# Attention plus mixture-of-experts layer on one core: the store of x2's rows moved behind the loads in the sync queue's step, and one Silu chunk of the shared layer moved ahead of the last tile's columns on ScalarE

## The reference

```
x = x + gamma * attention(layernorm(x), ctx, ctx)      # 8 heads, 4 batches of 512 rows x 512 columns
xn = layernorm(x)
shared = (silu(xn @ sw_gate) * (xn @ sw_up)) @ sw_down  # inner width 1408
routed = sum over the 2 best of 8 experts of their gated layer, weighted
x = x + routed + sigmoid(xn @ shared_gate_w) * shared
```

## Time and profile before

| what | value |
|---|---|
| median of 3 runs | 927.85 us (922.9 to 928.9) |
| the profiled execution | 931.65 us |
| its span, first to last instruction | 929.9 us |
| TensorE busy | 863.5 us, 93% of the span |
| VectorE, ScalarE, GpSimd busy | 570.5, 505.5, 442.8 us |
| attention stage | to about 289 us |
| shared layer | to about 650 us, routed experts to the end |

### The profile page before, as it was taken

The page is one execution under the profiler, slowest core; times in us unless marked ns, Lnnn a source line. Parts: engine busy times, 40 slices in busy tenths (PEclk is TensorE's granted clock), DMA queues, the critical chain, the costliest instruction groups (busy, mean ns, idle before and its releaser), DMA issues.

```text
span 929.9 us, 13754 instructions
## 1 busy us (share of the span) xinstructions
PE 863.5 (93%) x4624; PEld 715.8 (77%) x4624; DVE 570.5 (61%) x819; ACT 505.5 (54%) x862; POOL 442.8 (48%) x422
## 2 busy tenths in 40 slices
PE   4988898988986999999999999999999999999993
PEld 3666666666665888888888888888889999999992
DVE  4987888888762553442121212113989999999991
ACT  3886788778754332112111111112778888888881
POOL 5464666677450000004333000000589999999983
PEclk9998999999997999999999999999999999999996
DMA  9112223133234331400032002553945343434442
GB/s 104 47 35 86 85 80 135 57 113 113 80 125 136 103 102 46 136 1 1 2 136 25 1 0 91 187 187 105 336 103 91 69 89 69 83 75 83 76 68 35
DMA packets 63236, 81.24 MB, mean 87 GB/s; under 512 B 15369, under 2 KB 34825, under 8 KB 63186
## 3 DMA queue, kind: packets, MB, share of 16 engines
q1 hardware_dynamic: 53426, 60.14, 21.2%
q0 software_dynamic: 9760, 20.49, 12.3%
HBM read 53.01 MB, written 27.60 MB: 87 GB/s over the span
## 4 chain that ended last, share of the span: by engine, by line
PE 74%; POOL 11%; issue 7%; DVE 3%; ACT 2%; DMA 2%; POOLq 0%; SPq 0%; DVEq 0%; ACTq 0%
PE scores L1359 9%; PE scores L1360 9%; PE scores L1361 9%; PE bank L1373 4%; PE bank L1374 4%; PE bank L1375 4%; PE scores L1224 3%; PE bank L1459 3%; PE bank L1460 3%; PE bank L1461 3%; PE scores L1435 3%; PE scores L1437 3%; PE scores L1436 3%; PE bank L1435 3%; PE bank L1437 2%
## 5 line engine op out<-in xcount | busy, mean ns | idle before, releaser
L1016 DVE TENSOR_TENSOR sg<-scores,sg 128x512 f32<-128x512 f32 x44 | 30.4, 692 | 218.4 <-PE scores L1361 202.6
L1359 PE MATMUL scores<-x_hl,wsp 128*128 128x512 f32 x352 | 138.1, 392 | 0.0
L1360 PE MATMUL scores<-x_hl,wsp 128*128 128x512 f32 x352 | 137.8, 391 | 0.0
L1361 PE MATMUL scores<-x_hl,wsp 128*128 128x512 f32 x352 | 137.5, 391 | 0.0
L615 POOL DMA_INDIRECT slot_rows<-msrc,posi x32 | 36.1, 1129 | 184.6 <-PE scores L1361 178.2
L630 POOL DMA_INDIRECT xg<-x_normed_rows,meta x39 | 39.3, 1007 | 160.0 <-PE scores L1383 141.7
L789 ACT ACTIVATE sg<-scores 128x512 f32<-128x512 f32 x44 | 26.3, 598 | 160.2 <-PE scores L1361 160.2
L936 DVE TENSOR_TENSOR ptl<-bank,pth 128x512 fp32r<-128x512 f32 x128 | 87.7, 686 | 27.2 <-ACT pth L690 26.7
L690 ACT ACTIVATE pth<-bank 128x512 fp32r<-128x512 f32 x128 | 76.7, 599 | 43.2 <-PE bank L1233 42.5
L684 ACT ACTIVATE pb<-scores,negmax 128x512 f32<-128x512 f32 x128 | 88.1, 694 | 13.0 <-DVE negmax L926 13.0
L796 ACT ACTIVATE hh<-sg 128x512 fp32r<-128x512 f32 x44 | 27.8, 632 | 115.9 <-DVE sg L1016 100.9
(11 more groups left out here) (175 smaller groups left out, 2235.4 us busy)
## 6 DMA issues: line engine op xcount, KB each, us to landing
wex<-in_L_ffn_w_gate SPq DMA_DIRECT2D x8, 704.0 KB, 4.3
wex<-in_L_ffn_w_up SPq DMA_DIRECT2D x8, 704.0 KB, 6.1
xb<-in_x SPq DMA_DIRECT2D x16, 256.0 KB, 3.5
cn<-in_ctx SPq DMA_DIRECT2D x16, 256.0 KB, 3.0
x_rows<-xb SPq DMA_DIRECT2D x16, 256.0 KB, 2.0
x_normed_rows<-x2n SPq DMA_DIRECT2D x16, 256.0 KB, 2.3
x_normed_transposed<-x2T SPq DMA_DIRECT2D x16, 256.0 KB, 3.2
x_hl<-x_normed_transposed SPq DMA_DIRECT2D x4, 1024.0 KB, 5.2
```

The lines of the kernel that those rows point to most:

```text
L1359: te.matmul(bk[:, :], hi, xhi, start=(h == 0), stop=False)
L1360: te.matmul(bk[:, :], hi, xlo, start=False, stop=False)
L1361: ins = te.matmul(bk[:, :], lo, xhi, start=False, stop=(h == HC - 1))
```

## The change

In SyncE's step, `store_rows(i - 1)` moves from the first place to behind `load_x(i + 4)`. On ScalarE, `silu_hi(0, 0)` and `hidden_hi(0, 0)` move to between step 17 and step 18, ahead of the waits for the stores; the loop over the chunks leaves them out. Nothing is added or removed otherwise; the two helper functions are only defined earlier.

```
             def step(i):
-                if there(i - 1):
-                    store_rows(i - 1)
                 if there(i - 3):
                     store_normed(i - 3)
                 if there(i + 2):
                     paced(i - 1, 8)
                     load_values(i + 2)
                 if there(i - 3):
                     store_columns(i - 3)
                 if there(i + 4):
                     paced(i, 3)
                     load_x(i + 4)
+                if there(i - 1):
+                    store_rows(i - 1)
...
-            over_tiles(step)
+            for i in range(-4, NT + 2):
+                step(i)
+            silu_hi(0, 0)
+            hidden_hi(0, 0)
+            for i in range(NT + 2, NT + 3):
+                step(i)
...
             for c in range(SC):
-                silu_hi(0, c)
+                if c > 0:
+                    silu_hi(0, c)
                 if c + 2 < SC:
                     weights_hi(c + 2)
                 if c == 5:
                     tokens_hi(1, 1)
-                hidden_hi(0, c)
+                if c > 0:
+                    hidden_hi(0, c)
```

More of the change, by code:

```diff
@@ L769, in step @@
                     values_hi(i + 1)
[L770 to L780, removed]
             def silu_hi(b, c):
@@ L796, in hidden_hi @@
                 sc.activation(hh[p][:, :], sg[p][:, :], ACT.Copy).then_inc(a_hh, 1)
+            for i in range(-4, NT + 2):
+                step(i)
+            silu_hi(0, 0)
+            hidden_hi(0, 0)
+            for i in range(NT + 2, NT + 3):
+                step(i)
+            act.wait_ge(e_lg, NT)
+            act.wait_ge(g_x2n, NT)
+            act.wait_ge(a_lg, NT)
+            for q in range(2):
+                act.wait_ge(st_x2[q], 16 * NI)
+                act.wait_ge(st_x2n[q], 16 * NI)
+                act.wait_ge(st_x2T[q], 16 * NI)
+            act.wait_ge(st_pad, 32)
             for c in range(SC):
-                silu_hi(0, c)
+                if c > 0:
+                    silu_hi(0, c)
                 if c + 2 < SC:
```

## The result

| what | before | after |
|---|---|---|
| median | 925.38 us (920.69 to 928.9, 4 runs) | 897.67 us (896.54 to 899.42, 4 runs) |
| the profiled execution | 931.65 us | 899.42 us |
| its span | 929.9 us | 897.7 us |

The ratio is 0.9705, 95% interval 0.9652 to 0.9758: the changed kernel is 3% faster.

A forecast was written before the change was run, and what follows sets the result against it. Bound: an attention-stage loop through GpSimd, whose key cast waits 3.1 us for a late context load. Gains 27.2 + 2.4 = 29.6 us take the span from 929.9 to 900.3, 902.1 with surroundings; forecast 901 us, range 893 to 915.

The forecast's parts named there:

- The circle: Attention step's dependency loop through GpSimd, TensorE, ScalarE, VectorE: loses the 3.1 us context-load wait, 15.6 becomes 12.5 us.
- What is late next: a step of 13.95 us, TensorE bound: Attention stage: with GpSimd's load wait gone, TensorE's own work sets a step of about 13.95 us.
- The steps behind `first_tokens`: Four attention steps with more GpSimd work: low keys about 0.35 us late each, 1.4 us in all.
- The sum for the attention stage: 23.5 us of TensorE waits plus 5.1 for three slow-clock steps, minus 1.4: 27.2 us gained.
- The clock part: Attention stage: excess of three slow-clock steps, 5.1 us regained; bounds 0 to 5.1.
- The border: Between attention and experts: earlier Silu cuts TensorE's idle time from 7.19 to 4.8 us, 2.4 gained; range 0.7 to 5.4.
- I take zero: Behind the pause after the last logits: no change counted for half-speed products, where 3 us might return or 1.7 go.
- The low end of 893: Bottom of the forecast range: takes in the median's whole 3.8 us and a 5.4 us gain between attention and experts.
- The rival "VectorE becomes the bound": Attention stage: VectorE, busy 13.29 us a step, sets steps of 14.7 to 15 us; 915 or so; chance 0.15.
- The hidden load: Attention stage: GpSimd's next wait absorbs the gain or something equally long replaces it; 925 to 928 us; chance 0.08.
- GpSimd's collisions: Attention stage: moved GpSimd instructions each held 1.5 us by VectorE, making the kernel slower, about 945 us; chance 0.04.
- The rule on the shared ports: VectorE instructions with two SBUF inputs lock out GpSimd; large steady-step operations have at most one, so 13.95 us steps stay.

The follow-up runs named there:

- experiment 3: Kernel before with only the context tile's load moved ahead of the row store: 898.77 us, ratio 0.9728.
- experiment 4: Kernel before with the normed store, column store and load of x moved ahead of the row store, the context load left behind it: 913.1 us, ratio 0.9882.
- experiment 5: Kernel before with each tile's eight router-logit products issued twice: 925.95 us, ratio 1.0023.
- experiment 6: Changed kernel with each tile's eight router-logit products issued twice: 905.72 us, ratio 0.9803 against the kernel before.
- experiment 10: Changed kernel with VectorE's row statistics of x2 issued twice a step, the first into a spare tile: 897.95 us, ratio 0.9720 against the kernel before.
- experiment 7: Changed kernel with the two `first_tokens` instructions moved to where GpSimd waits for VectorE's variance: 894.43 us, ratio 0.9663 against the kernel before.
- experiment 2: Changed kernel with the row store back in its old place, so only the Silu's move against the kernel before: 921.7 us, ratio 0.9987.
- experiment 1: Kernel before with only the row store's move in SyncE's step, Silu in its old place: 899.02 us, ratio 0.9729.
- experiment 8: Changed kernel with the loads of weight chunks 2 and 3 issued before SyncE's step 18: 891.63 us, ratio 0.9635 against the kernel before.
- experiment 11: Kernel before with the row store's move and chunks 2 and 3 loaded before step 18, Silu in its old place: 894.27 us, ratio 0.9670.
- experiment 9: Changed kernel with `first_tokens` in GpSimd's gap, chunks 2 and 3 loaded and chunk 2 cast ahead of step 18: 888.43 us, ratio 0.9613 against before.

## Why the prediction was right

901 us was forecast with a range of 893 to 915; 897.67 was measured.

*The circle.* Right. The key cast's wait went to nothing, the waits for x2n vanished, and no slow-clock step is left between 66 and 232 us. Experiments 3 and 4 show that it is the context load and nothing else that SyncE's reordering moved; experiment 5 shows that TensorE had room before. The load went out 6.2 us into the step, where some 7 were forecast.

*What is late next: a step of 13.95 us, TensorE bound.* The mechanism was right (experiments 6 and 10), the size a little off: 13.61. I had taken TensorE's busy time from steps with waits, 13.91. In a step without waits it is 13.6; each of the two waits had added some 0.15 us to the busy time. The eight ordinary steps of before are 15.66 us in the mean, so each lost 2.05 us through its waits, of which the sum had counted only the time that TensorE stood idle, 1.77 in the mean. That is some 0.28 us too little in each of twelve steps, 3.4 us.

*The steps behind `first_tokens`.* The term was 1.4 us, at 0.35 each. They took 14.28 instead of 13.61, 2.7 us in all, so 1.3 us was missing here. The cause named was right, as experiment 7 shows. That 13.95 + 0.35 = 14.30 comes so near to 14.28 is luck: the two misses cancel.

*The sum for the attention stage* was 27.2; the two profiled executions differ by 29.65 between the row stores. With the two misses above it would have been 27.2 + 3.4 - 1.3 = 29.3. The clock part of 5.1 us is one of that execution: in experiment 2, with the old order, three steps took 16.1, 16.4 and 17.6 us instead of 19.6, 17.2 and 17.4, only the last of them with a clock below 1.00, and the stage 229.69 instead of 234.18. That is how the median moved by 27.7 us and the spans by 32.2, and probably in part why the runs of before scatter over 8 us and those of after over 3. By the medians the store's move brings 25.1 us (experiment 1) and not 27.2. So the closeness of 901 to 897.67 is partly luck: the waits were counted too low, the clock part is more than a usual execution loses, and the two err in opposite directions.

*The border.* 2.4 us were forecast, 2.2 us is the difference of the means over ten traces, and the two profiled executions differ by 1.72. TensorE idles 0.27 + 5.29 = 5.56 us there instead of the 4.8 forecast; chunk 2 landed 6.0 us after its first issue instead of 5.1, and between 5.1 and 5.8 in experiments 2, 6, 7 and 10; the trace doesn't say why. A stretch at the lower clock just ahead of the border is in both and cancels: from the last row store to the last column store 12.69 us after and 12.65 before, against 11.05 to 11.08 in experiments 1 to 4. "I take zero" for the clock behind the pause was right here, the products from 266.42 on ran at half speed too (0.63 us each), for 4.9 us where it had been 6.1. What the forecast did not have is that in experiments 2, 6, 7 and 10 the clock was down for the first down products already, as in experiment 2 above.

*The range.* The low end of 893 is 902.1 - 3.8 - 5.4, but 2.4 of the 5.4 are in the 902.1 already; its terms give 895.3. The measured median lies above either.

*The rival "VectorE becomes the bound"* fell with experiment 10. It had been argued from busy 13.29 of 15.70; with 13.5 of 13.6 the engine still held nobody up in these steps. *The hidden load* fell with experiments 1 and 3. *GpSimd's collisions:* the key cast takes 0.61 us after as before, x2n 0.76, so the moved instructions are not held. The rule on the shared ports was not put to a test of its own: VectorE's maximum at 157.88, which the prediction gave as agreeing, reads its input from PSUM, and none of VectorE's large operations beside the moved ones has two SBUF inputs.

## What to carry to other kernels

In a queue of transfers with waits of their own, a load that somebody needs early must not stand behind a store that waits for the end of the round. Look for an engine that is half idle and yet in the chain, and follow the chain once round. When a wait goes, take what is left from a step that has no waits: busy time beside a wait is too long. And where two waits end close together, taking one away may show little until the other goes as well; the traces of experiments 8 and 11 show this, the run times leave it open.

## What the runs showed of the hardware that was not expected

TensorE's busy time by the profile includes some 0.15 us per wait that isn't work: the same products take 13.9 us with two waits in the step, 13.7 with one (behind `first_tokens`) and 13.6 without. The rows of single products agree with it. Behind 302.6 in the kernel before a product's row is 0.39 us long while the next one starts after 0.23 us (302.66, 302.89); in front of a wait nothing covers the last 0.16 us of a row. These ends are modelled by the profiler, so this says how to read a profile and not how long the products really ran.

Two `BATCH_NORM_STATS2` in a row overlap a little by their rows: in experiment 10 the second started 0.61 us behind the first (95.35 and 95.96), though each row is 0.68 us long. Other VectorE instructions do so too (in the kernel after 134.03, 0.68 us long, and the next at 134.62). VectorE's busy time in a step rose by 0.46 us (13.06 to 13.52).

Whether a short wait brings TensorE's clock down differs between executions. Before, waits of 3.52, 1.85 and 2.01 us were each followed by a stretch at 1.2 GHz. In experiment 2 a wait of 2.25 us was, and those of 1.56 and 1.88 us were not; in experiments 4 and 5 none of up to 1.4 us in the steady steps was. But the stretch between the last two row stores has no wait over 1.3 us in any of the thirteen executions, and its end still ran at 1.2 GHz in before, after and experiments 7 and 9 (granted clock of the whole stretch 0.85 to 0.88), and at 1.00 in the nine others. The gap of 5.3 us in the kernel after was followed by half-speed products until 271.3, 4.9 us; the gap of 1.1 us in experiment 8 by none. The cause of these differences stays open.
